# A paged-attention layer chain on one core: where raw cache blocks land, when the masks are made, and the order of index products, maxima and copies

## The reference, cut to what matters

```python
x = x + einsum('bct,bcd->bdt', x, W0[cond])                          # L0: mix the 32 tokens of a sequence
x = x + x @ W.T + stop(scaling[a] * (x @ A[a].T) @ Bm[a].T)           # L1: dense layer and an adapter of rank 16
# L2: attention over a paged cache
q, k, v = x @ Wq.T, x @ Wk.T, x @ Wv.T           # 8 query heads, 4 key heads of 32
q, k = rope(rms(q, q_norm), pos), rope(rms(k, k_norm), pos)           # pos = kv_lens[:, None] + arange(32)
slot, off = pos // 16, pos % 16
blk = take_along_axis(block_tables, slot, axis=1)                     # tables may name a block more than once
k_blocks = k_blocks.at[blk, :, off, :].set(k)                         # the new rows go into the shared cache
v_blocks = v_blocks.at[blk, :, off, :].set(v)
k_all, v_all = k_blocks[block_tables], v_blocks[block_tables]
allowed = (kpos <= pos) & (kpos > pos - 128)
p = softmax(where(allowed, q @ k_all.T / 16, -inf))
x = x + (p @ v_all) @ Wo.T
x = x + x @ W3[id] + b3[id]                                           # L3: an expert per sequence
```

## Time and profile before

| | us |
|---|---|
| median of three timed runs | 164.01 (162.43 to 165.13) |
| profiled execution | 161.36 |
| its span, first to last instruction | 159.6 |
| TensorE busy | 117.0 (73%) |
| ScalarE busy | 86.0 (54%) |
| VectorE busy | 76.0 (48%) |
| GpSimd busy | 66.5 (42%) |

### The profile page before, as it was taken

How to read it: one execution, slowest core, us unless ns; L and a number is a source line. 1 busy time by engine, 2 the same in 40 slices (tenths; PEclk the granted TensorE clock), 3 DMA queues, 4 the chain that set the end, 5 groups by cost and what they waited for, 6 DMA issues and landing times.

```text
span 159.6 us, 3903 instructions
## 1 busy us (share of the span) xinstructions
PE 117.0 (73%) x1400; PEld 88.4 (55%) x1400; DVE 76.0 (48%) x306; ACT 86.0 (54%) x242; POOL 66.5 (42%) x83
## 2 busy tenths in 40 slices
PE   0276997889920399849377896949979796969873
PEld 0155957879400275439264675738566665756751
DVE  0579866488166308845804434343162625254131
ACT  3016661607239947347874997654566565658200
POOL 2677740294817756200001468836271423233300
PEclk9999999999997559999955699995999999999999
DMA  3994999998911549969229989989978787720000
GB/s 89 237 260 125 255 234 396 439 407 306 310 47 61 137 145 254 245 288 311 88 57 280 319 237 266 332 268 268 326 249 257 220 215 212 240 82 29 12 33 33
DMA packets 31323, 34.18 MB, mean 214 GB/s; under 512 B 6025, under 2 KB 29325, under 8 KB 29982
## 3 DMA queue, kind: packets, MB, share of 16 engines
q1 hardware_dynamic: 28424, 21.11, 46.1%
q0 software_dynamic: 2464, 12.29, 23.3%
q10 hardware_dynamic: 416, 0.54, 1.1%
HBM read 30.85 MB, written 7.18 MB: 238 GB/s over the span
## 4 chain that ended last, share of the span: by engine, by line
PE 31%; DMA 21%; POOL 18%; issue 12%; DVE 9%; ACT 6%; POOLq 1%; SPq 0%; DVEq 0%
DMA vm_m<-in_L_cond_k_blocks,tab_i 7%; PE bank L1071 6%; DMA blkp<-wr_rows,patch_i 6%; PE bank L1120 5%; PE bank L1133 4%; POOL xin_m L529 3%; DMA blkp<-in_L_cond_b,eid_i 3%; PE bank L1083 3%; POOL wr_rows L506 3%; PE bank L1053 3%; DMA lens_i<-in_itok_B 2%; PE bank L1128 2%; POOL tab_i L455 2%; PE bank L1107 2%; POOL vt_m L480 2%
## 5 line engine op out<-in xcount | busy, mean ns | idle before, releaser
L529 POOL TENSOR_TENSOR xin_m<-xin_m,ri 128x704 f32<-128x704 f32 x16 | 21.8, 1361 | 52.9 <-DVE ri L930 52.9
L688 ACT ACTIVATE xin_m<-kvn_m,nb 128x176 f32<-128x176 f32 x64 | 27.5, 436 | 7.4 <-DVE nb L938 7.4
L1071 PE MATMUL bank<-kt_m,natQ 32*64 32x176 f32 x256 | 15.1, 354 | 10.7 <-DVE nb L938 9.9
L938 DVE CUSTOM_DVE_ANT_0 kvn_m<-bank,mask 128x176 f32<-128x176 f32 x64 | 17.5, 330 | 4.6 <-PE bank L1071 4.6
L698 ACT COPY x_m<-bank 128x512 f32<-128x512 f32 x16 | 9.4, 588 | 16.8 <-PE bank L1083 16.7
L1071 PEld LDWEIGHTS bank<-kt_m,natQ 32*64 32x64 f32 x256 | 9.3, 146 | 15.4 <-issue 15.1
L1022 PE MATMUL bank<-wq_m,x_m 128*128 128x256 f32 x32 | 10.2, 482 | 10.4 <-ACT x_m L614 10.4
L1022 PEld LDWEIGHTS bank<-wq_m,x_m 128*128 128x128 f32 x32 | 7.6, 247 | 13.5 <-ACT x_m L614 12.0
L688 ACT ACTIVATION_READ_ACCUMULATOR xin_m<-kvn_m,nb 128x1 f32 x64 | 12.4, 193 | 0.0
L947 DVE TENSOR_TENSOR wq_m<-bank,blkp 128x256 f32<-128x256 f32 x8 | 3.4, 424 | 17.2 <-PE bank L1133 13.0
L1083 PE MATMUL bank<-cst,xin_m 128*128 128x128 f32 x64 | 11.0, 298 | 0.4 <-POOL xin_m L529 0.4
(11 more groups left out here) (191 smaller groups left out, 260.5 us busy)
## 6 DMA issues: line engine op xcount, KB each, us to landing
blkp<-in_L_cond_W SPq DMA_DIRECT2D x32, 256.0 KB, 3.6
v_rows<-blkp SPq DMA_DIRECT2D x3, 1024.0 KB, 9.6
wr_rows<-blkp SPq DMA_DIRECT2D x1, 1536.0 KB, 10.3
...
```

The lines of the kernel that those rows point to most:

```text
L529: pool.tensor_tensor(e_, e_, ri[:, p % 2, :].unsqueeze(2).broadcast_to([P, 4, KEYS]), ALU.mult).then_inc(s_pn, 1)
L688: act.activation(pr_seq(n % 2, u, j), S[:, n % 2, u, j, :], ACT.Exp, bias=nb[:, n % 2, 2 * u + j:2 * u + j + 1], scale=-1.0, accum_out=rs[ ...
L938: dve.tensor_tensor_reduce(S[:, n % 2, u, j, :], bank[2 + (2 * n + u) % 3][:, j * KEYS:(j + 1) * KEYS], mask[:, 2 * n + j, :], -SCALE, 3e3 ...
L1071: i_ = mm(bank[2 + (2 * p + u) % 3][GS * T * k:GS * T * k + GS * T, j * KEYS:(j + 1) * KEYS], QT[h, b // B4, b % B4, :], KT[h, b, :], star ...
```

## The change

1. Raw places. The writer unit's keys go to `kvn_m` (which held the mix weights until they were turned, so GpSimd waits for `s_mixt`) and its values to the place of the masks; before, both lay in `vt_m`. With this `vt_m` can be zeroed at the start: one half by GpSimd, one by ScalarE. `keep_k(0)` now waits until the writer keys are permuted. All gathers of table entries and blocks for the writer unit take 128 rows, not 96.
2. Masks. GpSimd computes all distances in one instruction of 128x1408 after the third block load (the other three loads of units 0 and 1 stand behind it), VectorE squares them and applies the threshold directly after the comparisons. `distance(n)` on ScalarE goes.
3. Order in front. On TensorE the index products stand after two tiles of the key projections instead of four; the third (`s_sel`) comes before half of the second key projection. On GpSimd the shift of row numbers comes before the loads of unit 2 and the expert sums. On ScalarE the mix copies come earlier, `idf` and some permutations later; unit 2 is permuted by VectorE, after the second half of the keys.
4. Loop. VectorE: maxima first, then `x3T`, reciprocal, result, copy of `oT`. The maxima now also wait for the exponentials of two steps before. The semaphore of the two copies of turned probabilities becomes two; both copies stay on ScalarE. The result is added one step later.

```diff
@@ raw places @@
+        mask_m = sb("mask_m", [P, B * KEYS // 2])
+        mask = mask_m[:, :].bitcast(BF16).rearrange("p (b r) -> p b r", b=B)
-        raw = {(NU, 0): vt_m[:, 0:RAW], (NU, 1): vt_m[:, RAW:2 * RAW], (0, 0): vm_m[:, 0:RAW], (0, 1): vm_m[:, RAW:2 * RAW],
+        raw = {(NU, 0): kvn_m[:, :], (NU, 1): mask_m[:, 0:RAW], (0, 0): vm_m[:, 0:RAW], (0, 1): vm_m[:, RAW:2 * RAW],
...
@@ gpsimd @@
+            pool.memset(vt_m[:, RAW:2 * RAW], 0.0).then_inc(s_vz, 1)
...
-                n = P if u < NU else NWI
+                n = P
...
-            for i in ((NU, 0), (NU, 1), (0, 0), (0, 1), (1, 0), (1, 1)):
+            pool.wait_ge(s_mixt, 1)
+            for i in ((NU, 0), (NU, 1), (0, 0)):
                 load_blocks(i)
             pool.wait_ge(s_len, 2)
             of_tokens(mid, rlen[:, :], C("in_tile"))
-            pool.tensor_scalar(mid[:, :], mid[:, :], -1.0, (WINDOW - 1) / 2, ALU.mult, ALU.add).then_inc(s_mid, 1)
-            pool.wait_ge(s_idf, 1)
-            of_tokens(eid, idf[:, :], None)
-            pool.sem_inc(s_eid, 1)
+            link(pool.tensor_scalar(mid[:, :], mid[:, :], -1.0, (WINDOW - 1) / 2, ALU.mult, ALU.add))
+            ptt(dist, C("iota").unsqueeze(1).broadcast_to([P, NT, KEYS]), mid[:, :].unsqueeze(2).broadcast_to([P, NT, KEYS]), ALU.add) \
+                .then_inc(s_dist, 1)
+            for i in ((0, 1), (1, 0), (1, 1)):
+                load_blocks(i)
...
-            for kv in range(2):
-                pool.wait_ge(s_perm[NU, kv], 1)
-            pool.memset(vt_m[:, :], 0.0).then_inc(s_vz, 1)
-            for kv in range(2):
-                pool.wait_ge(s_perm[0, kv], 1)
-                load_blocks((2, kv))
...
             pool.sem_inc(s_rowf, 1)
+            for kv in range(2):
+                pool.wait_ge(s_perm[0, kv], 1)
+                load_blocks((2, kv))
+            pool.wait_ge(s_idf, 1)
+            of_tokens(eid, idf[:, :], None)
+            pool.sem_inc(s_eid, 1)
@@ scalar @@
+            act.activation(vt_m[:, 0:RAW], ones[:, 0:1].broadcast_to([P, RAW]), ACT.Copy, scale=0.0).then_inc(s_vz, 1)
             act.activation(warm[:, 0:1], eps[:, 0:1], ACT.Sin)
...
+                if i == 0:
+                    act.wait_ge(s_perm[NU, 0], 1)
                 act.activation(ksq[:, 4 * i:4 * i + 4, :], b_, ACT.Square).then_inc(s_kk, 1)
...
-            def distance(n):
-                act.activation(dist[:, n, :], C("iota"), ACT.Square, bias=mid[:, n:n + 1]).then_inc(s_dist, 1)
@@ vector @@
+            dve.wait_ge(s_dist, 1)
+            step(stt(dist, dist, 1.0, dist, ALU.mult, ALU.mult))
+            ts(m4_own[:, :, :], dist, (WINDOW / 2) ** 2, -BIG, ALU.is_ge, ALU.mult).then_inc(s_m4, 1)
...
             k_part[1][1]()
-            dve.wait_ge(s_dist, NT)
-            ts(m4_own[:, :, :], dist, (WINDOW / 2) ** 2, -BIG, ALU.is_ge, ALU.mult).then_inc(s_m4, 1)
+            permute((2, 0))
+            permute((2, 1))
...
                     if n == 0:
                         dve.wait_ge(s_mask, 16 * B4)
-                        dve.wait_ge(s_patch[0], 16)
+                        dve.wait_ge(s_new, 16 * NT)
+                    if n >= 2:
+                        dve.wait_ge(s_exp, 4 * (n - 1))
@@ tensor @@
-            project_kv(0, 0)
             CNT = FLAT + NWI
+            project_kv(0, 0, (0, 1))
             pe.wait_ge(s_inr, 3)
...
-            project_kv(0, 1)
+            project_kv(0, 0, (2, 3))
             pe.wait_ge(s_can, 1)
...
-            project_kv(1, 0)
+            project_kv(0, 1, (0, 1))
             pe.wait_ge(s_val, 1)
...
+            project_kv(0, 1, (2, 3))
+            project_kv(1, 0)
             project_kv(1, 1)
```

106 lines of the change are left out of this document (50 added, 56 removed).

## The result

| | median of 4 runs | lowest to highest | profiled execution | its span |
|---|---|---|---|---|
| before | 164.57 us | 162.43 to 165.53 | 161.36 us | 159.6 us |
| after | 152.47 us | 150.61 to 155.31 | 155.31 us | 153.5 us |

The ratio is 0.9304, 95% interval 0.9113 to 0.9494: 7% less time.

The account below looks back on a forecast made before the run. GpSimd's late queue was taken to set the patch gather and so the attention's start, VectorE's order the loop's holes. Gains of 4.7 (front), 3.7 (gather) and 5.0 (loop), 13.4 us, gave 151 us, range 145 to 158.

Parts of the forecast that it names:

- The zeroing: Front: clearing vt_m at the program's start, half on GpSimd, half on ScalarE, hides behind other waits and costs nothing.
- The distances: Front: GpSimd sums distances from 18.5 to 21.2 while VectorE stands still on the shared port, a price of 2.6 us.
- The writer gathers: Front: gathers of 128 rows instead of 96 take longer; the second can cost 0 to 1.8 us, taken as 0.
- The shift: Front: GpSimd's shift of row numbers runs from 34.5 to 38.9 us, 5.9 us earlier than before.
- The scatters: Front: from 42.6 us they take 12.7 us plus 1.0 for VectorE collisions; patch gather issued at 56.3, gaining 4.7.
- rival B: Front: shared-port lock between GpSimd and VectorE takes 3.7 us of the gain, giving 154.3 us; chance 0.14.
- The patch gather: Front: without mask loads beside it, it lasts 6.0 us (5.0 to 9.7) instead of 9.7, gaining 3.7.
- The queries: Front, TensorE: first projection starts near 47.5, third ends near 59.3, ahead of the first turned keys by 3 us.
- The turning: Between the patch gather's landing and the first scores nothing changes: 12.3 us again.
- The loop: Loop over pairs: gains 5.0 us (1.3 to 6.5), 3.7 from maxima first and 1.3 around the experts' bias.
- Rival D: Loop: softmax chain becomes the limit, the reciprocal behind the maxima delaying GpSimd's multiply 1.04 us per step; 172 us, chance 0.03.
- Rival A: Loop: fed by the DMA, not VectorE, so it gains 1.5 us instead of 5, giving 154.1 us; chance 0.17.

Follow-up runs that it names:

- rows128: The kernel before with 128 instead of 96 rows in the writer unit's tables and gathers: 160.54 us, ratio 0.9946.
- again: The changed kernel itself, unaltered, measured and profiled once more: 151.91 us, ratio to the kernel before 0.9458.
- shift_alone: The changed kernel with VectorE turning the first keys behind the row indices, not beside GpSimd's row shift: 155.19 us, ratio to before 0.931.
- early_loads: The changed kernel with GpSimd issuing the last unit's two loads before the row shift: 149.66 us, ratio to before 0.9282.
- masks_behind_loads: The changed kernel with SyncE loading the masks only after the last unit's two loads have landed: 151.71 us, ratio to before 0.9475.
- early_filled: early_loads plus four products nobody reads on TensorE behind the third query projection: 149.53 us, ratio to the kernel before 0.9064.
- maxima_alone: The kernel before with only the maxima and their waits moved to the front of each VectorE loop step: 163.57 us, ratio 0.9882.
- loop_only: The kernel before with only the changed kernel's new VectorE order in the loop: 154.19 us, ratio 0.9602.

## Why the prediction was right or wrong

**The time.** 151 was forecast, 152.47 measured, and 151.91 in the repetition. The sum behind it was 8.4 us from the front and 5.0 from the loop. Taken apart on the chip the front gives 2.8 us (1.5 to 4.2) and the loop 6.4 (5.1 to 7.8). Two errors of opposite sign and unequal size are in it: the front was 5.6 us too good, the loop 1.4 too bad, so the whole was too good by some 4 us on the scale of the repetition and by 1.3 on that of the first measurement. That 151 lies so near 151.91 is in part luck: the sum starts from a kernel before at 164.01, and beside the repetition it took 161.8. By its own sign the account of the front was wrong: "a first score after 80 would make the prediction wrong whatever the loop does", and the first scores came at 84.70 and 81.53. The number held, the way to it did not.

**The zeroing** at the start, costed at nothing: right. GpSimd has done its half at 2.73 and then waits 0.89 us for the conditions; ScalarE's half takes 1.91 and a second table load 1.28, and ScalarE still waits 1.78 us for the first turned weights.

**The distances.** "18.5 to 21.2 on GpSimd", VectorE still for 2.6 us: measured 18.97 to 21.54, and a step whose neighbour takes 0.16 took 2.40. This agrees with the exclusive lock in the Trainium skill ("SBUF — State Buffer", section "SBUF: two separate sides"). The threshold was to end at 31.3 and ended at 31.16.

**The writer gathers** were costed at 0 within 0 to 1.8 us of loss. The sign was wrong: they gain at least 1.3 and 2.1 us (rows128). In the changed kernel that hid behind VectorE's standstill.

**The shift**, "34.5 to 38.9". Its start was right (34.30 in `again`; 36.60 in the first trace, by the clock at 29 to 36). Its length was not: 5.7 to 6.1 us instead of 4.4. I had put the first keys' rotation beside it on VectorE and applied the lock to copies and scatters only; shift_alone shows 4.4 once they are apart.

**From the shift to the scatters**, "2.5 for two loads, 0.9 for the sums, 42.6": measured 6.1 us from the shift's end to the first scatter. There is 0.87 of idle before the loads, the sums took 1.9 us beside VectorE's passes, and 1.08 stands before the first scatter. With the shift that is the 3.6 us by which `again` is late (46.17 against 42.6).

**The scatters**, 12.7 plus 1.0 for collisions: 13.6 in `again`, 14.0 in the first trace (stretches of 0.79, 0.62 and 0.33 beside VectorE's passes). Right; and rival B, the lock taking 3.7 us more, happened in part, though not at the scatters: 1.3 us at the shift and 1.0 at the sums.

**The patch gather**, "6.0, bounds 5.0 and 9.7": 6.8 to 7.2. Right in kind (12.2 with the masks beside it), 1 us too small. The step had a hole: "the patch window is free of them" was followed by no question about what the masks now ran beside. It is the last unit's loads, 12.6 and 14.4 us in `again` instead of 5.7 and 8.0.

**The queries**, "first projection near 47.5, third ends near 59.3, ahead by 3": the first was at 47.08 in `again` and 49.68 in the first trace, but the third ended at 68.85 and 66.5. The step counted ScalarE's work and left out that VectorE's copies of the last unit stand ahead of all the queries' sums and wait for a load. In `again` this is the step that set the first scores: the chain runs through it.

**The turning**, "nothing is changed: 12.3 us again": 14.7 us in the first trace and 15.0 in `again`, by two causes. In the first trace, in early_loads and in masks_behind_loads TensorE had stood idle (3.55, 4.78 and 5.81 us just before the landing, in the first trace 4.16 us shortly before that too) and turned the first keys at the lower clock; early_filled shows 1.87 against 3.49 us for the same products. I had noted in the earlier trace rows that the clock is at the lower level after an idle stretch, and used it for the queries only. Before, the third projection and its neighbours filled the time until the landing but for 2.0 us. In `again` the first keys were turned at the full clock but 2.1 us after the landing, behind the late queries, and 12.9 us passed from there.

**The front in sum**, in `again`: first scores at 81.53 against 74.6 (56.3, 6.0 and 12.3). Of these 6.9 us the way to the patch gather has 3.5, the gather 0.8 and the way from its landing to the scores 2.7.

**The loop**, "5.0, bounds 1.3 and 6.5", 7.1 us per two steps: 6.91 measured, and 6.4 us in time. Both terms of it were mis-sized, in opposite directions: 3.7 us for the maxima and 1.3 for the bias. By the timed runs the maxima alone gave 1.9 us (0.4 to 3.4) and the later places of the result, the sum for layer 3 and the copy the rest, some 4.5. Of the later places the result's is seen in the traces: 5.09 us of wait for the bias with the next maxima behind it in maxima_alone, 0.47 in loop_only. How the rest divides between the three places was not tried. The 0.3 us per place given back for the reciprocal is not seen. Rival D's delay of the reciprocal costs nothing in the first trace of after: TensorE waits for GpSimd there once, 0.42 us at 91.41.

**Rival A**, a loop fed by the DMA, does not cap the gain at 1.5 us. A weaker form of it is suggested and not shown: in four of the runs the chain from the landing runs over the values and SyncE's queue and ends some 81 us after the landing. No run changed SyncE's order or the values' way, so whether that is the next limit is open.
